# A transformer block with experts on one core: natural scores moved forward three tiles, projections and first scores among the last down projections

## The reference

```python
xn = _layernorm(x)
x = x + attn(xn) + ffn(xn)
# attn: q, k, v = split(xn @ w_in.T + b_in); 16 heads
scores = einsum('bhqd,bhkd->bhqk', q * scale, k) + causal_bias
out = einsum('bhqk,bhkd->bhqd', softmax(scores), v) @ w_out.T + b_out
# ffn: top 2 of 8 by softmax(xn @ gate_w.T), weights normed to 2.5
g = silu(xn @ w_gate[e]) * (xn @ w_up[e])          # F = 176 per expert
y = sum_e combine[:, e] * (g @ w_down[e])
y = y + (silu(xn @ sw_gate) * (xn @ sw_up)) @ sw_down   # 352 wide
```

## Time and profile before

| | |
|---|---|
| median of 3 runs | 666.92 us (666.62 to 674.36) |
| the profiled execution | 668.29 us |
| its span, first to last instruction | 666.6 us |
| PE busy | 571.7 us, 86% of the span, 4208 matmuls |
| DVE busy | 474.5 us, 71% |
| POOL busy | 358.6 us, 54% |
| ACT busy | 347.9 us, 52% |
| granted clock of TensorE, mean | 0.955 |
| PE's share of the chain that ended last | 63% |
| DVE's | 16% |

### The profile page before, as it was taken

The page is one execution under the profiler, slowest core; times in us unless marked ns, Lnnn a source line. Parts: engine busy times, 40 slices in busy tenths (PEclk is TensorE's granted clock), DMA queues, the critical chain, the costliest instruction groups (busy, mean ns, idle before and its releaser), DMA issues.

```text
span 666.6 us, 12739 instructions
## 1 busy us (share of the span) xinstructions
PE 571.7 (86%) x4208; PEld 324.8 (49%) x4208; DVE 474.5 (71%) x821; ACT 347.9 (52%) x472; POOL 358.6 (54%) x338
## 2 busy tenths in 40 slices
PE   1249989999799989999799988999899988989794
PEld 1136652556336643466336653466425663366422
DVE  4956967589756967479765988479664897569613
ACT  1422359533883448633693349634595338733482
POOL 3425726477257733478265754478154872568342
PEclk9658989999999988999999999999899999999879
DMA  6946004830247002850049001750039202670000
GB/s 162 267 104 165 1 7 97 195 75 16 55 127 189 16 6 51 179 133 16 21 109 239 16 6 47 188 128 16 6 95 213 54 16 53 143 176 16 7 1 17
DMA packets 44438, 57.12 MB, mean 86 GB/s; under 512 B 5936, under 2 KB 29840, under 8 KB 44240
## 3 DMA queue, kind: packets, MB, share of 16 engines
q1 hardware_dynamic: 44416, 56.83, 35.6%
HBM read 41.60 MB, written 15.20 MB: 85 GB/s over the span
## 4 chain that ended last, share of the span: by engine, by line
PE 63%; DVE 16%; issue 6%; DMA 5%; SPq 5%; ACT 4%; POOL 0%; DVEq 0%; POOLq 0%; ACTq 0%
PE banks L586 8%; PE banks L452 7%; PE banks L454 6%; PE banks L453 6%; PE banks L483 6%; PE banks L465 6%; PE banks L558 4%; PE banks L474 4%; PE banks L467 3%; PE banks L466 3%; DVE neg_max L1067 3%; ACT probs L768 2%; DMA k_op<-k_dram 2%; PE banks L608 2%; SPq L344 2%
## 5 line engine op out<-in xcount | busy, mean ns | idle before, releaser
L1067 DVE TENSOR_REDUCE neg_max<-banks 128x2 f32<-128x1024 f32 (+3 forms) x224 | 194.0, 915 | 39.1 <-PE banks L474 37.6
L855 POOL TENSOR_SCALAR_AFFINE_SELECT probs<-probs 128x512 f32<-128x512 f32 x128 | 92.8, 748 | 157.7 <-ACT probs L768 157.7
L768 ACT ACTIVATE probs<-banks 128x1024 f32<-128x1024 f32 x160 | 155.7, 1025 | 12.9 <-PE banks L558 10.7
L728 ACT ACTIVATE probs<-banks 128x512 f32<-128x512 f32 (+1 forms) x112 | 67.0, 598 | 163.8 <-PE banks L454 163.1
L822 POOL TENSOR_TENSOR probs<-probs,cb 128x512 f32<-128x512 f32 x88 | 116.3, 1322 | 67.0 <-ACT probs L728 54.7
L828 POOL TENSOR_TENSOR hid_lo<-probs,hid_hi 128x512 fp32r<-128x512 f32 (+1 forms) x96 | 123.2, 1284 | 52.7 <-ACT hid_hi L736 51.8
L586 PE MATMUL banks<-probs,v_op 128*32 128x512 f32 (+3 forms) x1024 | 97.0, 452 | 0.2
L452 PE MATMUL banks<-x_hi,w_hi 128*128 128x512 f32 (+1 forms) x224 | 93.5, 417 | 2.7 <-DVE w_lo L1203 2.7
L736 ACT ACTIVATE hid_hi<-probs 128x512 fp32r<-128x512 f32 (+1 forms) x112 | 69.5, 628 | 39.8 <-DVE probs L1049 39.6
L454 PE MATMUL banks<-x_hi,w_lo 128*128 128x512 f32 (+1 forms) x224 | 90.0, 402 | 0.0
L453 PE MATMUL banks<-x_lo,w_hi 128*128 128x512 f32 (+1 forms) x224 | 89.5, 400 | 0.0
(11 more groups left out here) (113 smaller groups left out, 644.1 us busy)
## 6 DMA issues: line engine op xcount, KB each, us to landing
cb<-c_dram SPq DMA_DIRECT2D x32, 256.0 KB, 7.8
q_op<-q_dram SPq DMA_DIRECT2D x32, 192.0 KB, 5.6
k_op<-k_dram SPq DMA_DIRECT2D x32, 192.0 KB, 6.2
cb<-c_dram SPq DMA_DIRECT2D x16, 224.0 KB, 8.1
q_dram<-q_parts SPq DMA_DIRECT2D x16, 192.0 KB, 2.7
k_dram<-k_parts SPq DMA_DIRECT2D x16, 192.0 KB, 2.7
cb<-c_dram SPq DMA_DIRECT2D x16, 192.0 KB, 7.9
cb<-c_dram SPq DMA_DIRECT2D x16, 160.0 KB, 6.4
```

The source lines that it names most:

```text
L768: nc.scalar.activation(probs[:, g % 2, 2 * u:2 * u + 2, :], ring[:, 2 * (n % 2):2 * (n % 2) + 2, :], ACT.Exp).then_inc(exp_done, 1)
L855: return nc.gpsimd.affine_select(out=view, in_=view, compare_op=ALU.is_ge, fill=0.0, base=0, pattern=[[0, 4], [1, P]], channel_multiplier=-1)
L1067: return nc.vector.tensor_reduce(out, in_, AX.X, ALU.max, negate=True)
```

## The change

The list of pairs per step and the slots: pairs 0 and 1 of the next block go into attention, and steps 0 to 10 take the other 18, where steps 2 to 12 took 20. Pairs 0 to 5 all use the slot of banks 3 and 4, from pair 6 on both slots are used in turn. The transposes and the output projection that were in `bank_m` during the first steps move to `nat[:, 0]` (bank 5), the logits from `bank_y` to `bank_m`, the transposed y from `bank_m` to `bank_y`. The buffers of the hidden tiles inside `probs` are renumbered, so that the buffers that exp writes first hold no hidden tile. The two halves of the ring change places in `scores_t`. The maxima are transposed at step 12 instead of 13. `logits`, `project_q`, `project_v`, `scores_t(0,0)` and `scores_t(0,1)` move in among the last two down projections. The exp table is called behind the last silu. Attention in the first turn waits for the low parts of the last tiles, since exp writes over their buffers. No instruction is added to or taken from the sum of the work, and the order on SyncE and GpSimd is the same. In the diff, the first `experts_and_maxima` and `attend` are TensorE's, the second ones VectorE's, and `experts` is ScalarE's.

```diff
-PAIRS_AT = [(int(2 <= k <= 12), int(4 <= k <= 12)) for k in range(16)]
-SPARE_FROM = 4
+AHEAD = 2
+PAIRS_AT = [1 if k < 4 else 2 if k < 11 else 0 for k in range(NT + 2)]
+ONE_SLOT = AHEAD + 4
 def pair_slot(n):
-    return (n - SPARE_FROM) % 2 if n > SPARE_FROM else 0
+    return n % 2 if n >= ONE_SLOT else 1
...
-        hid = probs[:, 0, 0:3, :]
-        sg = probs[:, 0, 3:6, :]
+        hid = [probs[:, 0, n, :] for n in (4, 6, 2)]
+        sg = [probs[:, 0, n, :] for n in (5, 7, 3)]
+        o_banks = [bank_y, bank_m, bank_y, banks[:, 5, :]]
...
             def gate_up(b, k):
-                    pe.wait_ge(exp_done, ST_ALL * b - 1 + k)
+                    pe.wait_ge(exp_done, ST_ALL * b)
...
             def scores(b, i, g, v):
                     pe.wait_ge(ops_loaded[n // (NAT_ALL // 2)], OP_LOADS * 16 * b + OP_LOADS * 16)
                 if n == 0:
-                        pe.wait_ge(o_taken, GROUPS * b)
-                elif n == SPARE_FROM + 1:
-                    pe.wait_ge(silu_done, NT * b + 1)
-                    pe.wait_ge(hid_done, NT * b + 1)
-                    pe.wait_ge(combT_done, b + 1)
+                        pe.wait_ge(exp_done, ST_ALL * i + ST_ALL - 1)
+                        pe.wait_ge(o_normed, GROUPS * i + 2)
+                elif n == ONE_SLOT:
                         pe.wait_ge(tail_step, 3 * i + 1)
...
             def scores_t(i, g, u):
                     pe.wait_ge(m_loaded, 32 * i + 32)
+                    pe.wait_ge(silu_done, NT * i + NT)
+                elif n == 1:
                     pe.wait_ge(hid_done, NT * i + NT)
-                    bank = ring[:, 2 * (n % 2) + a, :]
+                    bank = ring[:, 2 * ((n + 1) % 2) + a, :]
...
             def experts_and_maxima(b, i, front):
-                n = 0
+                n = 0 if i is None else AHEAD
-                    if k == NT and front:
-                        project_k(b + 1)
+                    if k == NT - 2:
+                        transpose_maxima(b)
+                        if front:
+                            transpose_x(b + 1)
+                    if k == NT:
+                        if front:
+                            project_k(b + 1)
+                            logits(b + 1)
+                        scores_t(b, 0, 0)
+                    if k == NT + 1:
+                        if front:
+                            project_q(b + 1)
+                        scores_t(b, 0, 1)
                     if k >= 2:
                         down(b, k - 2, i)
-                    if k == 13:
-                        transpose_maxima(b)
-                        if front:
-                            transpose_x(b + 1)
+                if front:
+                    project_v(b + 1)
...
             def attend(i, front):
+                        if (g, u) == (0, 3):
+                            transpose_y(i)
+                            if g == GROUPS and u in (1, 3):
+                                pair(i + 1, i, u // 2)
...
             def experts(b, i, front):
                     if k == NT - 1:
+                        nc.scalar.activation(table_call[:, :], bqk[:, 1:2], ACT.Exp)
+                    if k == NT - 2:
                         act.wait_ge(mT_ready, b + 1)
...
             def experts_and_maxima(b, i, front):
-                    if k == 12:
+                    if n == NAT_ALL and PAIRS_AT[k]:
                         split_maxima(b)
-                    if k == 12 and front:
-                        normalise(b + 1)
+                        if front:
+                            normalise(b + 1)
+                if front:
+                    router_logits(b + 1)
                 for k in range(NT - LATE, NT):
                     low_hidden(b, k)
...
             def attend(i, front):
+                if front:
+                    split_k(i + 1)
+                    take_v(i + 1)
                 add_tokens(i)
...
                 take_o(i, 2)
+                if front:
+                    pair(i + 1, 0)
                 normalise_o(i, 2)
+                if front:
+                    pair(i + 1, 1)
```

More of the change, by code:

```diff
@@ L414, in project_v @@
             def project_v(j):
-                before(pe, base_done, j)
+                pe.wait_ge(router_step, ROUTER_STEPS * j + 2)
                 for q in range(QT):
@@ L459, in down @@
                 pe.wait_ge(hid_lo_done, NT * b + k + 1)
-                if k == 0:
-                    pe.wait_ge(router_step, ROUTER_STEPS * b + 2)
-                    if i is not None:
-                        pe.wait_ge(o_normed, GROUPS * i + 3)
+                if k == 0 and i is not None:
+                    pe.wait_ge(o_normed, GROUPS * i + 3)
                 hi, lo = hid_hi[0:n, k % 3, :], hid_lo[0:n, k % 3, :]
@@ L493, in scores @@
                 if n == 0:
-                    if isinstance(b, int) and b == 0:
+                    if i is None:
+                        pe.wait_ge(combT_done, 1)
+                    else:
+                        pe.wait_ge(exp_done, ST_ALL * i + ST_ALL - 1)
+                        pe.wait_ge(o_normed, GROUPS * i + 2)
+                elif n == ONE_SLOT:
+                    if i is None:
                         pe.wait_ge(q_done, 1)
@@ L523, in transpose_maxima @@
                 pe.wait_ge(msplit_step, 4 * b + 4)
-                before(pe, tail_step, 3 * b)
-                pe.wait_ge(combT_done, b + 1)
                 apart(pe, pe_passed)
@@ L632, in experts_and_maxima @@
                         transpose_o(i, 3, True)
-                    for _ in range(sum(PAIRS_AT[k])):
-                        scores(b, i, n // NAT_PAIRS, n % NAT_PAIRS)
+                    for _ in range(PAIRS_AT[k] + (AHEAD if k == 0 and i is None else 0)):
+                        pair(b, i, n)
                         n += 1
-                    if k == NT and front:
-                        project_k(b + 1)
+                    if k == NT - 2:
[11 more added lines that the diff above has]
+                        scores_t(b, 0, 1)
                     if k >= 2:
@@ L643, in experts_and_maxima @@
                         project_out(i)
-                    if k == 13:
-                        transpose_maxima(b)
-                        if front:
-                            transpose_x(b + 1)
+                if front:
+                    project_v(b + 1)
             def attend(i, front):
-                transpose_y(i)
                 for g in range(GROUPS + 1):
                     for u in range(UNITS):
-                        if g < GROUPS:
+                        if g < GROUPS and (g, u) not in ((0, 0), (0, 1)):
                             scores_t(i, g, u)
+                        if (g, u) == (0, 3):
+                            transpose_y(i)
                         if front and g == GROUPS and u in (2, 3):
@@ L1135, in finish_output, with pair @@
                 nc.vector.copy_predicated(base[:, :, :], not_nan[:, :, :], both[:, :, :]).then_inc(tail_step, 1)
+            def pair(b, n):
+                maxima(b, n // NAT_PAIRS, n % NAT_PAIRS)
             def experts_and_maxima(b, i, front):
-                n = 0
+                n = 0 if i is None else AHEAD
                 for k in range(NT + 1):
@@ L1147, in experts_and_maxima @@
                         normalise_o(i, 3)
-                    for _ in range(sum(PAIRS_AT[k])):
-                        maxima(b, n // NAT_PAIRS, n % NAT_PAIRS)
+                    for _ in range(PAIRS_AT[k] + (AHEAD if k == 0 and i is None else 0)):
+                        pair(b, n)
                         n += 1
-                    if k == 12:
+                    if n == NAT_ALL and PAIRS_AT[k]:
                         split_maxima(b)
-                    if k == 12 and front:
-                        normalise(b + 1)
+                        if front:
+                            normalise(b + 1)
                     if k == 6 and i is not None:
```

88 lines of the change are left out of this document (40 added, 48 removed).

## The result

The changed kernel takes 754.44 us in the median (752.41 to 757.61, 4 runs) where the kernel before takes 666.77 (665.59 to 674.36, 4 runs): a ratio of 1.129, 95% interval 1.120 to 1.139. The forecast was 744 us, 712 to 768, slower. Some executions of a kernel fall into a slower state, whatever the kernel; all medians, ranges and ratios here leave them out.

A forecast was written before the change was run, and what follows sets the result against it. TensorE was taken to set the pace, busy 69.05 of 75.38 us per block. Terms of 10.2 us per transition, 71 over seven, plus 5 for block 0 and 1 for the last drain gave 744 us, range 712 to 768.

The forecast's parts named there:

- wait for the operands: Tail of attention: TensorE reaches pair 0 before its q and k transfers land and stands 5.9 us per block.
- pairs 2 and 3 in one slot: Pairs 0 to 5 share banks 3 and 4, so pairs 2 and 3 wait for reductions: +3.15 us per turn.
- the old 1.39 us wait: Wait between two pairs sharing one pair of banks; it goes, as pairs 6 and 7 have two slots: -1.39 us.
- waits of the drain: End of the experts: 5.4 us of waits against 4.4, including 2.75 before gate and up of tile 12: +1.0.
- clock: TensorE resumes at half clock behind the transfer wait, sized by block 0: 1.5 us per turn, bounds 0 and 2.8.
- rival B: Operands come earlier or waits overlap more: 720 us, or 691 if wholly in time; chance 0.13.
- Rival C: Drain filled as drawn, its 4.4 us of waits per transition go: faster, 653 us without transfer wait; chance 0.04.
- The ends: Block 0, with three pairs at step 0, costs +5 us (bounds 3 and 8); the last block's drain +1.

The follow-up runs named there:

- experiment 1: The kernel before plus one wait for the operands' first half, ahead of gate and up in the tail of attention: 729.8 us, ratio 1.088.
- experiment 2: The changed kernel without reloading q_op and k_op, so blocks 1 to 7 use block 0's operands: 697.67 us, ratio 1.047.
- Experiment 3: The changed kernel with the reductions of pairs 1 and 2 reading a quarter of their elements: 732.78 us, ratio 1.096.
- Experiment 4: The changed kernel without the reload of q_op and k_op and with the reductions of pairs 1 and 2 cut short: 670.69 us, ratio 1.006.
- slots_norm: The kernel before with the change's banks, slots, hidden-tile buffers and their waits, and the next block's normalise at VectorE's step 3: 664.73 us, ratio 0.994.
- norm_early: The kernel before with only the next block's normalise moved from step 12 to step 3 of VectorE's experts: 662.58 us, ratio 0.991.
- experiment 6: The changed kernel with VectorE's split of the maxima and normalise at step 11, behind hidden(10): 748.44 us, ratio 1.116.

## Why the prediction was right, and where its terms were off

The start of each block's store of the maxima gives the period: over seven turns it grew from 76.39 to 88.24 us, 11.85 more where I had 10.2. Term by term, per turn:

| term | predicted | measured |
|---|---|---|
| wait for the operands | 5.9 | 6.1 (48.3 less block 0's 5.6, over 7) |
| pairs 2 and 3 in one slot | 3.15 | 2.71 |
| the old 1.39 us wait | -1.39 | -1.39 |
| waits of the drain | +1.0 | +1.34 (5.77 against 4.43) |
| clock | 1.5 | 3.6 (24.9 us of PE busy over the seven periods) |

The measured terms add to 12.3, 0.5 over the period's growth: PE's idle time grew by 8.3 us a period where the four waiting terms make 8.8, so small idles that the table leaves out went away.

**The operand wait** came as drawn: TensorE at the wait as the last transfer is issued, 5.77 us of idle in the turn shown (5.74 to 6.38 in the seven), and the same chain ahead of it. The fit that rival B cites (the Trainium skill, DMA: Bandwidth & Descriptors, "Anatomy of one DMA — SWDGE (gpsimd) path") is given there for transfers that GpSimd issues; SyncE issues these, and the last of the four landed 5.8 us after its issue. Experiments 1 and 2 show the term from both sides, 8.7 and 8.1 us a turn with its clock.

**The slots** were right in place and number and 0.4 too dear. Each of the two waits is 1.32 to 1.39 us and not 1.5; I had the row of 1.39 and reckoned above it. Experiment 3 showed that the reductions end them.

**The drain.** Waits of the same size did stand elsewhere, the largest at gate and up of tile 12 (3.02, predicted 2.75). Experiment 4 leaves 2 to 4 us for drain, table load and block 0 together, and block 0 alone is 4.1 of the change (below), so the drain's net cost is near nothing. Rival C's gain of 4.4 a turn is nowhere. Of the 4.43 us of waits before, 1.90 were for VectorE and 2.53 for ScalarE; the change moved VectorE's split and norm in front of more of its own products, and the wait appeared there.

**The clock is the term that was mis-sized**, 1.5 us a turn where the runs show 3.6. The step took one drop per turn, behind the long wait, at the size of block 0's. There are three in most turns, behind the 3.0, the transfer's wait and the pair of slot waits, and in four of seven a fourth at the start of attention. The earlier trace rows has a wait of 1.39 with the clock at 1.00 all through the earlier trace rows, and from that block I took waits of this size as free. For a wait of 1.39 alone that is so: the clock is 1.00 behind it in all seven later blocks of the kernel before. The low clock at 250 there follows the drain's waits of 1.19 to 0.69. What was not in any row is two such waits 2 us apart, in a turn that has two longer ones. 2.1 us a turn, 14.5 in all, is the miss.

**The ends.** From the start to block 0's store of the maxima the time grew by 4.1 us (forecast +5), and from the last store to the end it fell by 2.4 (forecast +1), which makes +1.8 where I had +6. (The store stands a step earlier in the changed kernel.) In block 0 the wait is 5.57 us and slot waits of 1.39 and 1.33 follow, as said. With the seven turns that is 84.7 of span against 77. The median lies 3.1 above the profiled span, and not 0.3. That makes the 10 us between 744 and 754.4.

That the miss is no larger is in part luck: the clock alone was 14.5 us short, and the slots, the ends and the idles left out took 11 of that back.

The Trainium skill (TensorE: Matmul & The Clock Gate, "A second HAM failure mode: psum-queue depth-cycling") says that short idles between groups of matmuls that cycle through PSUM banks can suffice to make the clock swing. I had leaned on the section about waits for transfers alone. The rows here agree with both: 2.3 us of clock behind each transfer wait (experiment 1), and 7.8 us in all that went with the slot waits (experiment 3).

**What stays open:** why the clock falls in one block and not in the next for the same waits. slots_norm has 1.09, 0.69 and 0.69 us of idle in its drain and runs at 0.50 from 324 to 332; norm_early, in its fastest execution, has 1.19, 0.69 and 0.69 there and stays at 1.00, and it stays there behind six waits of 1.66 too. No run isolates it.

## What to carry to other kernels

Before work is moved forward on an engine that runs in order, read when its inputs land: here the last transfer is issued as the engine arrives, and the work that used to hide the flight was queued behind the wait. Price a long wait on a busy TensorE as more than the wait: here one of 6.3 us cost 8.7. Count the waits of one to three microseconds as well where several stand in a turn; one of 1.39 us alone cost no clock. And ask whose lateness a gap shows: two of the five gaps at the experts' end were VectorE's, and moving one norm of 1.1 us to an earlier step of VectorE brought 5.8 us, where rearranging TensorE's queue brought nothing.

## What the runs showed of the hardware that was not expected

- Low clock follows waits of 1.9 and 3.0 us as it follows one of 5.8 (0.72, 0.57 and 0.50 in the stretch behind), and a pair of 1.3 to 1.4 us waits in five of seven turns. Behind a single wait of 1.39 (the kernel before) or 1.66 (norm_early) it was 1.00 each time, and behind the drain's waits of about 1 us it is low in some blocks and not in others.
- A VectorE operation on 128 x 64 numbers takes 0.19 to 0.23 us alone and 1.07 to 1.33 us when it begins while one of GpSimd's products of 1.3 us is running; it then ends within 0.1 us of it (352.37 and 352.32, 353.63 and 353.55, 354.82 and 354.77 in experiment 6). The Trainium skill (SBUF — State Buffer, "SBUF: two separate sides") describes an exclusive lock of the port pair that the two engines share, held for a whole instruction, against VectorE operations in a two-port mode and against those with two inputs in SBUF when GpSimd's operation reads SBUF; the trace agrees, for the casts and for the subtraction.
- The exp table's load is 1.28 us, with the call directly behind, in the new place as in the old.
